# A perceiver layer on one core: transposed router rows kept for the shared network, router logits with 8 moving columns, and an expert product between two shared products

## The chip, the core and the metric

The kernel runs on one core of a Trainium2 chip. Its engines are PE (TensorE: matrix products and transposes, into eight PSUM banks), DVE (VectorE), ACT (ScalarE), POOL (GpSimd) and SP (SyncE, which here issues most DMAs). Each engine works through its own instructions in order and waits for counters (semaphores) that the others raise. The metric is the device time of one execution, in microseconds (us).

## What is computed

The input is x, 32 batches of 64 tokens with 512 features, and a context of 32 x 1601 rows. Three residual blocks follow each other: an attention over the context, a causal self-attention of 16 heads, and a feed-forward block with a router, experts and a shared network. The change touches the third block and its seam with the second:

```python
x = x + xattn(layernorm(x), ctx)
x = x + attn(layernorm(x))
h = layernorm(x)
logits = h @ w_router.T                  # 8 experts
weight, idx = top_k(softmax(logits), 2)  # weights made to sum to 1
moe = sum over the two chosen experts of weight * (square(relu(h @ w1[e].T)) @ w2[e].T)
shared = square(relu(h @ ws1.T)) @ ws2.T # 1024 inner features
out = x + shared + moe
```

## The kernel before

The 2048 tokens are T = 16 tiles of 128. P = 128, D = 512, KD = D / P = 4, KF = 1024 / P = 8, E = 8, TR = 12 and TA = 12. The order of every engine's work is written out by hand; semaphores join them.

Router: for each tile DVE writes the normalised rows to `hs[i]` (line 1027), PE transposes them (`router_T`, line 1912, four transposes recorded at line 1702), ACT copies them from PSUM to `h2Tr[i]`, one of two buffers (`router`, line 833, recorded at line 716), and PE multiplies with the router's weights, stored with 120 columns of zeros (`router`, line 2023, the tile's rows being the stationary operand and 128 columns moving). Tiles TR to T-1 have buffers of their own (`h2T_late`), since the shared network takes them at the very end of the kernel.

Shared network for tiles 0 to 11, in six pairs p: DVE normalises each tile again (`norm_c`), PE transposes it again (`tokens_T_c`), ACT and DVE make high and low parts from PSUM (`h2_high`, `h2_low`). PE computes four groups g of 256 inner features (`shared_first`, 24 records a group) into banks 1 to 4. ACT applies relu (`relu_of`), DVE squares, ACT and DVE split into `shT_p` (`shared_high`, line 921, and `shared_low`, line 1460). PE multiplies with ws2, one tile after the other (`shared_second`, 24 records each), into bank 5 for even tiles and bank 6 for odd ones, and DVE adds the bank to x (`residual_c`, line 1466, counter `x3_ready`). The second half of a pair runs after the first half of the next pair. `shared_second` of a tile waits until `residual_c` of the tile two before has read its bank. ACT's first `shared_high` of pair p waits for `shared_done` >= 2p, since `shT_p` is one buffer.

Between these, DVE computes the routing (lines 1542 to 1604) and the rows are scattered to `moe_in` by POOL (line 697).

Experts: 39 tiles of routed tokens. SP loads a tile's tokens (`load_slots`, line 553, four DMAs), the low parts of w1 and w2 of the tile's expert (`load_low`, line 533; `load_low2`, line 539); the rest of the weights is resident (`load_w1`, `load_w2`) and is loaded while the shared network runs. DVE transposes the tokens (`tokens_T`, line 1529), ACT and DVE split them. On PE `experts(g)` transposes the squared values of tile g-1, makes the first product of tile g (lines 2147 to 2156) and then the second product of tile g-1 (the same lines). On DVE, `tokens_T(g+1)` stands ahead of the square of tile g.

On SP, before: after the last attention product (`out_done`) it loads w1 of experts 2 to 7, then stores h2T of the late tiles, then w1 of expert 1, then x of tiles 0 to 3 and 4 to 7 away (line 519, each followed by weights that take the place), then x of tiles 12 to 15 (line 526); it waits for that store (line 530), loads low parts for tile 0, w1 of expert 0, the tokens of tile 0, six experts' worth of w2 and, once tile 0 is transposed, the tokens of tile 1.

## Time and profile before

| | |
|---|---|
| median of 3 runs | 1371.45 us (1368.12 to 1372.08) |
| profiled execution | 1369.75 us |
| its span, first to last instruction | 1368.0 us |
| PE busy | 1324.4 us, 97% |
| DVE busy | 719.2 us, 53% |
| ACT busy | 341.6 us, 25% |
| granted TensorE clock, mean | 0.995 |
| share of PE in the chain that ended last | 87% |
| share of SP's issue and of DMAs in that chain | 6% and 3% |

All times in the text are microseconds from the start of the span of this profiled execution. PE's busy time is split in products and weight loads (PEld), which overlap. A row of the timeline gives start, duration, engine, line and operation, the operands, the number of instructions merged in it, and in brackets the idle time before it with what ended it. A row of the chain of waits gives start, duration and the work that the end of the span waited for. The granted clock 1.00 is 2.4 GHz and 0.50 is 1.2 GHz.

### The profile page before, as it was taken

The numbers are of one execution on the slowest core, as the hardware profiler recorded it, in microseconds if no ns is written. First come the engines' busy times: TensorE is split into PE (matmuls) and PEld (weight loads), VectorE is DVE, ScalarE is ACT, GpSimd is POOL, SyncE is SP. The second block draws the span as 40 slices with busy tenths as digits, with TensorE's granted clock in tenths as the row PEclk, the third lists the DMA queues.
The fourth block names the chain that finished last, engine by engine and source line by source line (L and its number), as shares of the span: only waits on it lengthen the run. The fifth ranks groups of instructions, "written<-read, shape, count | busy, mean of one in ns | idle before, by whom it ended". The sixth has DMA issues, their size and how long they took to land.

```text
span 1368.0 us, 20895 instructions
## 1 busy us (share of the span) xinstructions
PE 1324.4 (97%) x7251; PEld 818.1 (60%) x7252; DVE 719.2 (53%) x1353; ACT 341.6 (25%) x604; POOL 160.6 (12%) x169
## 2 busy tenths in 40 slices
PE   5889999999999999999999999899998999999999
PEld 2334444444444444357888888799896666666643
DVE  3235444544444444467877786757442444444436
ACT  2101111211111111234444443442121222222210
POOL 0000000000000000003000005502330000000045
PEclk9999999999999999999999999999999999999999
DMA  9999999999999999721466752062549998999887
GB/s 360 392 401 395 396 394 395 395 394 384 383 381 379 379 379 352 297 82 76 157 252 256 271 211 97 35 222 80 192 153 310 295 302 283 298 291 293 273 323 257
DMA packets 122945, 392.18 MB, mean 287 GB/s; under 512 B 12144, under 2 KB 34672, under 8 KB 122768
## 3 DMA queue, kind: packets, MB, share of 16 engines
q1 hardware_dynamic: 117776, 374.79, 75.0%
q0 software_dynamic: 5120, 16.78, 3.4%
q8 instruction: 26, 0.43, 0.1%
q14 instruction: 23, 0.19, 0.0%
HBM read 333.32 MB, written 58.20 MB: 286 GB/s over the span
## 4 chain that ended last, share of the span: by engine, by line
PE 87%; SPq 6%; DMA 3%; DVE 2%; issue 1%; ACT 1%; POOL 0%; DVEq 0%; POOLq 0%; ACTq 0%
PE ps L1801 12%; PE ps L1865 12%; PE ps L1741 10%; PE ps L1855 10%; PE ps L2147 7%; PE ps L1702 4%; PE ps L1762 4%; PE ps L1754 4%; PE ps L1751 4%; PE ps L2153 3%; PE ps L2150 3%; PE ps L2156 3%; PE ps L2222 2%; PE ps L2214 2%; SPq L393 2%; DMA arena<-ctx_t 2%
## 5 line engine op out<-in xcount | busy, mean ns | idle before, releaser
L716 ACT ACTIVATE arena<-ps 128x512 f32<-128x512 f32 (+1 forms) x151 | 79.9, 542 | 602.2 <-PE ps L1702 278.6
L1801 PE MATMUL ps<-arena 128*64 128x512 f32 (+1 forms) x832 | 193.6, 597 | 0.5 <-DMA arena<-ctx_n 0.5
L1741 PE MATMUL ps<-arena 128*64 128x512 f32 (+1 forms) x1024 | 178.9, 503 | 11.9 <-DMA arena<-ctx_t 8.9
L1865 PE MATMUL ps<-split 128*128 128x256 f32 x1344 | 170.1, 285 | 0.1
L1855 PE MATMUL ps<-split 128*128 128x512 f32 x672 | 163.8, 396 | 4.3 <-DVE split L1460 2.3
L1865 PEld LDWEIGHTS ps<-split 128*128 128x128 f32 x1344 | 163.5, 191 | 6.1 <-issue 5.2
L1741 PEld LDWEIGHTS ps<-arena 128*64 128x64 f32 x1024 | 66.3, 137 | 133.1 <-issue 119.9
L1855 PEld LDWEIGHTS ps<-split 128*128 128x128 f32 x672 | 123.1, 188 | 34.4 <-issue 3.1
L1140 DVE SCALAR_TENSOR_TENSOR arena<-arena,hbar 128x512 f32<-128x512 f32 x128 | 90.5, 749 | 94.7 <-PE ps L1762 89.9
L1801 PEld LDWEIGHTS ps<-arena 128*64 128x64 f32 (+1 forms) x832 | 58.4, 138 | 114.4 <-issue 112.2
L1073 DVE TENSOR_REDUCE small<-ps 128x1 f32<-128x1601 f32 x16 | 29.2, 1825 | 141.3 <-PE ps L1741 141.3
L2150 PE MATMUL ps<-split 128*128 x195 | 90.0, 559 | 0.0
L2147 PE MATMUL ps<-arena 128*128 x156 | 73.3, 592 | 0.9 <-ACT split L974 0.9
L1529 DVE STREAM_TRANSPOSE zero<-arena 128x512 uint32<-128x512 uint32 x39 | 27.7, 711 | 81.2 <-PE ps L2156 57.7
L635 POOL COPY arena<-arena 128x512 f32<-128x512 f32 x16 | 9.7, 609 | 495.5 <-PE ps L1723 490.2
L708 POOL DMA_INDIRECT arena<-moe_out,slot_i x32 | 33.2, 1037 | 295.7 <-DMA moe_out<-arena 286.3
L1762 PE MATMUL ps<-arena 128*64 128x512 f32 x256 | 66.0, 594 | 0.0
L1702 PE MATMUL ps<-ident,arena 128*128 128x128 f32 x368 | 54.6, 280 | 10.0 <-DVE arena L1027 9.7
L1751 PE MATMUL ps<-arena 128*128 128x512 f32 x128 | 60.2, 614 | 1.9 <-DMA arena<-w_qv 1.9
L2150 PEld LDWEIGHTS ps<-split 128*128 128x128 f32 x195 | 37.4, 192 | 39.3 <-issue 37.6
L1754 PE MATMUL ps<-arena 128*128 128x512 f32 x128 | 57.6, 593 | 1.9 <-DVE arena L1127 1.9
L2153 PE MATMUL ps<-split 128*128 x195 | 58.3, 397 | 0.0
(180 smaller groups left out, 1681.1 us busy)
## 6 DMA issues: line engine op xcount, KB each, us to landing
arena<-ctx_t SPq DMA_DIRECT2D x128, 800.5 KB, 19.1
arena<-ctx_n SPq DMA_DIRECT2D x128, 768.0 KB, 15.7
split<-parts_low SPq DMA_DIRECT2D x39, 768.0 KB, 7.3
split<-parts_low SPq DMA_DIRECT2D x39, 512.0 KB, 5.2
moe_in<-zero SPq DMA_DIRECT2D x3, 3328.0 KB, 13.5
arena<-moe_in SPq DMA_DIRECT2D x156, 64.0 KB, 3.9
moe_out<-arena SPq DMA_DIRECT2D x39, 256.0 KB, 4.7
stage_raw<-w1t SPq DMA_DIRECT2D x8, 768.0 KB, 5.5
```

The source lines that it names most:

```text
L1140: v.scalar_tensor_tensor(Wc[:, h, :], w_qv_sb[:, 3 * KD + k, :], hbar[:, k, h:h + 1], w_qv_sb[:, k, :], ALU.mult, ALU.add).then_inc(wc_rea ...
L1702: last = nc.tensor.transpose(dst[:, P * k:P * (k + 1)], src[:, P * k:P * (k + 1)], ident[:, :])
L1741: last = mm(bank(n)[S * h:S * (h + 1), 0:w], qT[:, k, S * h:S * (h + 1)], ctxT[h][:, k, at_j:at_j + w], start=(k == 0), stop=(k == KD - 1))
L1751: mm(bank(5), F2[:, k, :], w_qv_sb[:, KD + k, :], start=(k == 0), stop=False)
L1754: mm(bank(5), F3[:, k, :], w_qv_sb[:, 2 * KD + k, :], start=False, stop=False)
L1762: last = mm(bank(5)[r, :], F1[i][:, k, r], Wc[:, h, :], start=False, stop=(k == KD - 1))
L1801: last = mm(bank(7)[S * h:S * (h + 1), :], ET[0:w, c, S * h:S * (h + 1)], ctxN[h][0:w, c, :], start=(c == 0), stop=(c == JC - 1))
L1855: last = mm(dst, lhs[a][:, k, :], rhs[b][:, k, :], start=(k + i == 0), stop=(k == n - 1 and i == 2))
L1865: last = mm(dst[:, 2 * P * m:2 * P * (m + 1)], w[a][:, k, c], tokens[b][:, k, :], start=(k + i == 0), stop=(k == KD - 1 and i == 2))
L2147: mm(dst, raw(k), raw_w(k), start=(k == n), stop=False)
L2150: mm(dst, parts[0][:, k, :], high_w(k), start=False, stop=False)
L2153: mm(dst, parts[1][:, k, :], high_w(k), start=False, stop=False)
```

## The change

What it does, part by part:

- The transposed rows of tiles 0 to 11 are kept: tiles 0 and 1 in `h2T_first`, tiles 2 to 11 in `h2T_rows`, where w1 of experts 2, 3 and half of 4 will lie. `norm_c` and `tokens_T_c` are gone, and `h2_high` and `h2_low` read the kept rows. Pair 1 has buffers of its own for its high and low parts.
- The router's products move 8 columns instead of 128, and the logits of tiles 0 to 11 share bank 3; they are copied out twice instead of four times.
- The router's work for tiles 12 to 15 stands between the groups of the shared network's first pair.
- SP loads w1 of experts 2, 3 and 4 later, one by one: expert 2 after the first store of x, 3 and 4 after the second.
- On PE `experts(0)` comes between the second products of tiles 10 and 11. In tile 11's product (`shared_last`) the passes with the low part of the tokens come first, and then SP may load the next low part of w1 over them. PE waits for all w1 before `experts(0)`.
- On DVE the last pair's squares and subtractions all come ahead of `residual_c` of tile 8; that of tile 9 comes after the transposing of expert tile 0, that of tile 11 after that of expert tile 1.
- On SP the tokens of tile 1 are loaded ahead of the last four w2 instead of behind them, and after the last shared product the tokens of tile 2 are loaded ahead of the low parts of w2.

```diff
+        h2T_first = [within(f"h2T_first{i}", 2 * KD * D + 2 * D + i * D, KD, P) for i in range(2)]
+        h2T_rows = within("h2T_rows", SPLIT, TR - 2, KD, P)
...
-        low_lo = ARENA + TR * D, used[0], used[0] + KA * D
+        low_lo = ARENA + TR * D, 8192 + 9216 - KA * D, used[0]
...
-        def logits(g):
-
-            return bank(3 + 2 * (g % 2))
+        def logits(lo, hi):
+
+            return bank(3 if hi <= TR else 0)[:, E * lo:E * hi]
...
@@ SP
-            load_w1(2, E)
+            load_w1(5, E)
...
                 if i == 0:
+                    sp.wait_ge(h2lo_ready, 6)
+                    load_w1(2, 3)
                     sp.wait_ge(routed, EXPERTS)
                     load_w2(3 * KD * D, 3, 4)
+                else:
+                    sp.wait_ge(h2lo_ready, 10)
+                    load_w1(3, 4)
+                    sp.wait_ge(h2lo_ready, TA)
+                    load_w1(4, 5)
...
             load_slots(0)
             load_w2(0 * KD * D, 0, 2)
+            sp.wait_ge(xgT_ready, 1)
+            load_slots(1)
             load_w2(4 * KD * D, 4, 6)
             load_w2(2 * KD * D, 2, 3)
-            sp.wait_ge(xgT_ready, 1)
-            load_slots(1)
+            e = expert_of(1)
+            sp.wait_ge(shlo_used, 1)
+            load_low(e, 1)
             sp.wait_ge(shared_done, TA)
+            load_slots(2)
             load_low2(0, expert_of(0))
-            load_low(expert_of(1), 1)
-            load_slots(2)
             load_low(expert_of(2), 2)
@@ ACT
             with act.Fori(3, TR // 2 - 1) as n:
                 for i in range(2):
-                    router(2 * n + i, i, False)
+                    router(2 * n + i, i)
+            act.wait_ge(out_done, T)
             for i in range(2):
-                h2_high(0, i, True)
+                h2_high(0, i)
             for i in range(2):
-                router(TR - 2 + i, i, False)
+                router(TR - 2 + i, i)
+            for i in range(2):
+                h2_high(1, i)
             sqrt_of_var(7, TR, T)
             relu_of(0, 0, True)
             relu_of(0, 1, True)
+            for i in range(2):
+                router(TR + i, i, late_bank[i])
             shared_high(0, 0, True)
...
@@ DVE
-            shared(4, norms=False, scatter=6)
-            shared_start(TA // 2 - 1, more=False, norms=False)
+            shared(4, scatter=6)
+            last_pair = TA // 2 - 1
+            square(last_pair, 0)
+            square(last_pair, 1)
+            shared_low(last_pair, 0)
+            square(last_pair, 2)
+            shared_low(last_pair, 1)
+            square(last_pair, 3)
+            shared_low(last_pair, 2)
+            shared_low(last_pair, 3)
+            residual_c(TA - 4, 0)
             dve.wait_ge(slots_zeroed, 48)
-            shared_rest(TA // 2 - 1)
             tokens_T(0)
             tokens_low(0)
-            for i in range(2):
-                residual_c(TA - 2 + i, i)
+            residual_c(TA - 3, 1)
+            residual_c(TA - 2, 0)
...
-            experts(0, True, False, True)
+            experts_square(0)
+            tokens_T(1)
+            tokens_low(1)
+            residual_c(TA - 1, 1)
@@ PE
-            def router(t, i):
+            def router(t):
 
                 pe.wait_ge(r_h2T_ready, t + 1)
-                src = h2T_late[t - TR] if t >= TR else h2Tr[i]
                 for k in range(KD):
-                    last = mm(logits(t // KD)[:, P * (t % KD):P * (t % KD + 1)], src[:, k, :], wr_sb[:, k, :],
+                    last = mm(logits(t, t + 1), h2T_of(t)[:, k, :], wr_sb[:, k, 0:E],
                               start=(k == 0), stop=(k == KD - 1))
                 last.then_inc(lg_done, 1)
...
+            def shared_last(p):
+
+                pe.wait_ge(x3_ready, 2 * p)
+                high, low = (a[:, :, P:2 * P] for a in shT_p)
+                for k in range(KF):
+                    last = mm(bank(6), low[:, k, :], ws2_p[0][:, k, :], start=(k == 0), stop=False)
+                last.then_inc(shlo_used, 1)
...
+            shared_group(0, 0, first=True)
+            shared_group(0, 1, first=True)
+            router_T(TR, 0, False, late_bank[0])
+            router_T(TR + 1, 1, False, late_bank[1])
+            pe.wait_ge(lg_read, 1)
+            shared_group(0, 2, first=True)
+            router(TR)
+            router_T(TR + 2, 0, False, late_bank[0])
+            router(TR + 1)
+            router_T(TR + 3, 1, False, late_bank[1])
+            shared_group(0, 3, first=True)
+            router(TR + 2)
+            router(TR + 3)
+            shared_first(1)
...
-            for i in range(2):
-                shared_second(TA // 2 - 1, i)
-            pe.wait_ge(w1_in, 16 * 6)
+            shared_second(TA // 2 - 1, 0)
+            pe.wait_ge(w1_in, 16 * 12)
             pe.wait_ge(relu_ready, 4 * (TA // 2) - 2)
             experts(0, now=(0, 0))
+            shared_last(TA // 2 - 1)
             experts(1, now=(1, 0), last=0, second=True)
```

## Rows read from the trace of the kernel before

**Rows 1.** The page, busy time, share of span and instructions of each engine.

```profile
PE 1324.4 (97%) x7251; PEld 818.1 (60%) x7252; DVE 719.2 (53%) x1353; ACT 341.6 (25%) x604; POOL 160.6 (12%) x169
```

**Rows 2.** The chain of waits, router stretch: start, duration, what.

```profile
880.57 1.78 PE ps L2023 x16
...
897.08 1.31 PE ps L1702 x12
...
899.28 0.44 PE ps L1702 x4
```

**Rows 3.** The timeline of PE around the first late tile.

```profile
912.91 1.91 PE L1702 MATMUL ps<-ident,arena 128*128 128x128 f32 x16
915.26 1.13 PE L2023 MATMUL ps<-zero,arena 128*128 128x128 f32 x8 [0.45 <-ACT arena L716]
```

**Rows 4.** The chain of waits through the pairs.

```profile
955.26 0.87 PE ps L1702 x8
...
967.03 11.51 PE ps L1865 x96
...
1025.18 10.92 PE ps L1855 x48
```

**Rows 5.** The timeline of weight loads, two windows around the first two of a run.

```profile
871.17 0.30 PEld L2023 LDWEIGHTS ps<-zero,arena 128*128 128x128 f32 x2
...
875.40 0.20 PEld L1702 LDWEIGHTS ps<-ident,arena 128*128 128x128 f32 x2 [1.23 <-DVE arena L1027]
```

**Rows 6.** Stretches: length, busy PE, PEld, DVE, ACT, POOL, clock, DMA share, GB/s.

```profile
873.57:876.98 3.41, 1.57 (x32) 1.19 (x28) 3.38 (x6) 1.65 (x2) 3.33 (x3) 1.00 0.00 0
876.98:880.39 3.41, 3.41 (x16) 3.03 (x16) 3.29 (x5) 1.79 (x3) 3.25 (x4) 0.50 0.00 0
893.10:900.70 7.60, 7.60 (x70) 7.60 (x69) 5.25 (x15) 4.30 (x8) 0.37 (x3) 1.00 0.81 315
1057.88:1061.30 3.42, 3.42 (x8) 2.33 (x7) 0.42 (x1) 0.06 (x1) 0.00 (x0) 0.50 0.72 235
```

**Rows 7.** The timeline of ACT, one copy of transposed rows.

```profile
898.52 0.60 ACT L716 ACTIVATE arena<-ps 128x512 f32<-128x512 f32 x1
```

**Rows 8.** The chain of waits, last shared products and first expert steps.

```profile
1041.67 0.69 DVE split L1460
...
1065.29 0.44 PE ps L1702 x4
...
1071.75 0.44 PE ps L1702 x4
1072.18 0.86 PE ps L2147 x2
...
1075.12 1.72 PE ps L2147 x4
```

**Rows 9.** The timeline of DVE and PE in the same stretch.

```profile
1030.76 0.69 DVE L1466 TENSOR_TENSOR arena<-arena,ps 128x512 f32<-128x512 f32 x1 [8.51 <-PE ps L1855]
...
1037.69 1.62 PE L1855 MATMUL ps<-split 128*128 128x512 f32 x6 [1.60 <-DVE split L1460]
...
1056.59 0.66 PE L1702 MATMUL ps<-ident,row_a 128*128 128x128 f32 x4 [3.55 <-DVE row_a L1640]
```

**Rows 10.** The timeline of SP's queue: issues of token loads.

```profile
1030.31 2.77 SPq L553 DMA_DIRECT2D arena<-moe_in  x4
...
1055.17 1.75 SPq L553 DMA_DIRECT2D arena<-moe_in  x4
```

**Rows 11.** DMAs: low parts of w2 on the page; landing times of line 553.

```profile
split<-parts_low SPq DMA_DIRECT2D x39, 512.0 KB, 5.2
...
DMA to landing us min/median/max: 2.4/5.3/10.5
```

**Rows 12.** SP's waits; last, a stretch with line 1702's busy times, clock, DMA, GB/s.

```profile
SPq L530 <- DMA x_away<-arena: 6.6, 1, 6.6
...
1013.70:1037.00 23.30, 0.00 (x0) 0.00 (x0) 1.00 0.81 277
```

More of the change, by code:

```diff
@@ L219, in perceiver_layer @@
         shT_p = [as_split(carve(KF, 2 * P)) for _ in range(2)]
-        h2T_p = [as_split(carve(KD, 2 * P)) for _ in range(2)]
+        h2T_p = [[as_split(carve(KD, 2 * P)) for _ in range(2)]]
+        h2T_p.append([])
+        for lo in (4 * KD * D, 2 * KD * D + 2 * D):
+            at(lo)
+            h2T_p[1].append(as_split(carve(KD, 2 * P)))
         relu = [row_a[:, :], row_b[:, :]]
@@ L229, in perceiver_layer @@
         hs = [carve(D) for _ in range(2)]
-        h2Tr = [carve(KD, P) for _ in range(2)]
+        carve(2, D)
         assert used[0] == 3 * KD * D, used[0]
@@ L831, in exp_probs, with router @@
                                      ACT.Exp).then_inc(p_ready, 1)
-            def router(t, i, first, source=None):
+            def router(t, i, source=None):
                 act.wait_ge(r_h2T_done, t + 1)
-                if not first:
-                    act.wait_ge(lg_done, t - 1)
-                dst = h2T_late[t - TR] if isinstance(t, int) and t >= TR else h2Tr[i]
-                copy(dst.rearrange("p a b -> p (a b)"), source or bank(1 + i)).then_inc(r_h2T_ready, 1)
+                nc.scalar.activation(h2T_of(t), (source or bank(1 + i)).rearrange("p (k n) -> p k n", n=P), ACT.Copy
+                                     ).then_inc(r_h2T_ready, 1)
             def round_set(n):
@@ L899, in _, with h2_high @@
             for i in range(2):
-                router(4 + i, i, False)
+                router(4 + i, i)
             attn_high(T - 1, 1, False)
-            def h2_high(p, i, first):
-                act.wait_ge(h2T_done, 2 * p + i + 1)
-                if not first:
+            def h2_high(p, i):
+                act.wait_ge(r_h2T_ready, 2 * p + i + 1)
+                if not isinstance(p, int):
                     act.wait_ge(sh_done, 4 * p)
-                nc.scalar.activation(h2T_p[0][:, :, P * i:P * (i + 1)],
-                                     bank(7 * i).rearrange("p (k n) -> p k n", n=P), ACT.Copy).then_inc(h2hi_ready, 1)
+                nc.scalar.activation(h2T_of_pair(p)[0][:, :, P * i:P * (i + 1)], h2T_of(2 * p + i), ACT.Copy
+                                     ).then_inc(h2hi_ready, 1)
             def relu_of(p, g, first=False):
@@ L951, in _ @@
             for i in range(2):
-                h2_high(1, i, False)
-            for t in range(TR, T):
-                router(t, t % 2, False, late_bank[t % 2])
+                router(TR + 2 + i, i, late_bank[i])
             relu_of(0, 3)
@@ L1474, in _ @@
                 router(TR + i, i)
-            copy_logits(2)
             for i in range(2):
-                norm_c(2 + i, i)
+                h2_low(1, i)
             square(0, 0)
             square(0, 1)
+            for i in range(2):
+                router(TR + 2 + i, i)
             shared_low(0, 0)
@@ L1482, in _ @@
             shared_low(0, 1)
-            for i in range(2):
-                h2_low(1, i)
-            for i in range(2):
-                router(TR + 2 + i, i)
             square(0, 3)
@@ L2047, in _ @@
             probs_T(T - 1)
-            router(2, 0)
-            router(3, 1)
+            router(2)
+            router(3)
             attend_b(T - 1, 1)
@@ L2098, in shared_second, with shared @@
                            arrived if i == 0 else None).then_inc(shared_done, 1)
-            def shared(p, second=False, more=True):
+            def shared_last(p):
[4 more added lines that the diff above has]
+                last.then_inc(shlo_used, 1)
+                for k in range(KF):
+                    for part in ws2_p:
+                        last = mm(bank(6), high[:, k, :], part[:, k, :], start=False,
+                                  stop=(k == KF - 1 and part is ws2_p[1]))
+                last.then_inc(shared_done, 1)
+            def shared(p):
                 shared_first(p)
                 for i in range(2):
-                    if more:
-                        tokens_T_c(p + 1, i)
-                for i in range(2):
-                    shared_second(p - 1, i, second)
+                    shared_second(p - 1, i)
             pe.wait_ge(ws1_split, 4 * KD)
-            shared_first(0, first=True)
-            for i in range(2):
-                tokens_T_c(1, i)
-            for t in range(TR, T):
-                if t == TR + 1:
-                    pe.wait_ge(relu_ready, 1)
-                router_T(t, t % 2, False, late_bank[t % 2])
-                if t == TR + 1:
-                    pe.wait_ge(relu_ready, 3)
-                if t > TR:
-                    router(t - 1, 1 - t % 2)
-            router(T - 1, 1)
-            shared_first(1, second=True)
+            shared_group(0, 0, first=True)
[12 more added lines that the diff above has]
+            shared_first(1)
             pe.wait_ge(routed, MASK)
@@ L2136, in _ @@
                 shared(p)
-            shared(TA // 2 - 1, more=False)
+            shared(TA // 2 - 1)
             def expert(g):
```

131 lines of the change are left out of this document (55 added, 76 removed).

## The prediction, made before the changed kernel had run

> **What bounds the kernel now.** I read the page first: PE is busy for 97% of the span [rows 1], so work taken from PE counts wherever no other engine ends the stage. The change touches 870 to 1085 us, so I then read the chain of waits there. To 1036.1 us it is PE nearly without a break: router products and transposes first [rows 2], then per pair of token tiles 96 products of line 1865, 8 transposes and 48 products of line 1855 [rows 4]. A microsecond of PE work removed there comes off the end. From 1036.1 to 1057.4 us the chain leaves PE: first for the split of the last pair's squared values on ACT and DVE, then for a load of expert tokens (line 553). From 1065 us each of the 39 expert tiles takes 6.46 us of PE [rows 8].
>
> **Removed: twelve second transposes.** Every tile of the shared network was normalised and transposed a second time, four transposes in 0.44 us [rows 2]. Two tiles stand in the run of 12 transposes at 897.08, two in the 16 at 912.91, and two, 0.87 us, in each of the next four pairs [rows 2 to 4]. All lie on the chain: 12 x 0.44 = 5.2 us. DVE also loses the second normalisations, off the chain, worth nothing. The rounding copies and subtractions stay, now reading SBUF.
>
> **Reordered: the last four tiles' router work.** It now lies between groups of line 1865. After the 16 transposes at 912.91 PE waited 0.45 us for an ACT copy, and the products that followed took 1.13 us where eight take 0.89 (half of 1.78) [rows 2, 3]: 0.7 us, which 2.88 us of shared products per group (11.51/4 [rows 4]) now cover. So far 5.9 us. Covers: ACT's two rounding copies now stand ahead of its copies of tiles 10 and 11, two more of 0.6 us [rows 7] in a stretch where ACT is busy for 4.3 of 7.6 us [rows 6]; without that cover PE would wait up to 1.2 us. The split of ws1 on POOL ends well before. The routing arithmetic on DVE begins with PE's logits and moves with them, behind 11.5 us of shared products as before.
>
> **Router products with 8 columns instead of 128: nothing.** There are 16 tiles of 8 records, now 0.11 us apart (16 in 1.78 us [rows 2]). Their streaming falls to almost nothing, but each keeps its 128-column weight load. Two such loads at the head of a run took 0.30 us in all and 0.19 each, so the second began 0.11 us after the first, before a product could hold it; two loads for transposes took 0.20 and 0.14, 0.06 apart [rows 5]. A record therefore stays at 0.11 us. Bounds: 0.06 us (the transpose's load) would give 14 x 8 x 0.05 = 5.6 us on the chain (tiles 0 and 1 lie in idle time); the 0.12 us of line 1865 (11.51/96) would cost 1.1. I take nothing: the loads of this very line show the limit.
>
> **TensorE's clock in the router stretch: a loss.** From 893.1 to 900.7 us PE is now busy throughout at the full clock [rows 6]. Afterwards it streams only five tiles' transposes there, 2.2 of 7.6 us, and otherwise loads weights. The clock stood at half, 1.2 GHz, from 877.0 to 880.4 after 3.4 us in which PE was busy for 1.57, and from 1057.9 to 1061.3 after idle time [rows 6, 9]. I expect one fall, with 3.4 us at half rate: 1.7 us lost. Bounds: no fall, or two such stretches (3.4 us lost).
> The Trainium skill ("TensorE: Matmul & The Clock Gate", Part 4) says that transposes do not count as busy for the clock. The trace is against it: from 877.0 to 880.4 PE ran nothing but transposes, and the clock rose at the end of it [rows 6]. By the rule the fall would be sure and hold to the end of the stretch, its second 3.8 us of work taking 7.6, 3.8 us lost; by the row it is only likely.
>
> **The last shared products and the first expert: a loss too.** Before, from 1036.10 to the transposes of the third expert step at 1065.29 is 29.2 us [rows 4, 8]. Afterwards, on the same time axis:
> DVE now runs all squares and subtractions of the last pair ahead of the residual addition of tile 8, which ran at 1030.76, as soon as the bank was full [rows 9]. PE may not write bank 5, tile 10's product, until that addition is done. The chain of squares cannot start sooner than before, since ACT's first copy still waits for both products of pair 4 (1036.1), and DVE's last subtraction ends at 1042.36 [rows 8]. Then 0.69 us of addition: PE starts at 1043.05 instead of 1037.69 [rows 9]. A wait of 6.95 us, with all of PE's later work queued behind it.
> Then: 24 products 5.46 (half of 10.92 [rows 4]); a clock fall, as there was after 3.55 us idle at 1056.59 [rows 6, 9], 1.7; the first expert product 2.94 (1072.18 to 1075.12 [rows 8]), its tokens ready by 1045; tile 11's product 5.46; the second expert step 6.46. Sum 28.97.
> SP then is late. Its token loads for step 3 were issued at 1055.17, before the step that began at 1056.59 [rows 9, 10], and the low parts of the first w2 before them. Now both follow the last shared product, tokens (1.75 us of issue) first, and the low parts, with a register load between, go out about 3 us into the second step. They land 5.2 us after issue [rows 11], at 8.2, where PE wants them at 6.2. Step 3's tokens are delayed alike, and DVE transposes them ahead of the square that PE needs. I take 2.5 us for both (bounds 0.4, if the emptier queues land in 4 us, and 4.5). Result 31.5 against 29.2: 2.3 us lost. The 3.55 us of idle time and 1.9 us of slow clock that expert 0's product now covers are gone; late instead is the bank.
>
> **Weights reloaded later on SP.** The kept rows cover the places of experts 2, 3 and half of 4, so three loads of 1 MB move behind the stores of x. Two are queued ahead of the store whose wait of 6.6 us holds SP [rows 12]. 2 MB at 277 GB/s [rows 12] are 7.2 us, and 1.7 us of issue: the first token loads go from 1030.31 [rows 10] to at most 1039.2 and at the median of 5.3 us [rows 11] land at about 1047, ahead of the first expert product at 1050.2. Hidden, with 1 to 3 us to spare after transpose and split; past that each microsecond costs one.
>
> **Sum.** -5.9 (transposes, waits) + 0 (columns) + 1.7 (clock) + 2.3 (transition) = -1.9 us. Against the profiled 1369.75 that is 1367.9; the median of the runs shown is 1371.45, 1.7 above it, so 1369.5. This kernel's measurement tells 0.3%, 4.1 us, from no change.
>
> **Rivals.**
> A, the clock does not fall in the router stretch. For: the records follow each other as closely as before. -3.6: 1367.8. Chance 0.22; with shorter waits for SP it passes 4.1 in half the cases.
> B, a router record takes 0.06 us. For: two transposes' loads lay so. Against: the two loads of this line did not. -1.9 - 4.8 (of the 5.6, ACT's copies of 0.6 us a tile [rows 7] take some back): 1364.7. Chance 0.10. The same page of the Trainium skill ("Back-to-back issue gap") puts a product of few columns at a floor of 25 ns, by which the gain would be some 9 us, and its section on LDWEIGHTS a 128-column load at 107 ns, by which it is none; the loads above side with the second.
> C, the transition gains: PE does not wait for bank 5, so neither the 2.3 us lost nor the old 5.4 us remain: -9.6, 1361.8. Against: the order of DVE's instructions. Chance 0.08.
> D, the first tokens come late because of the reloaded weights. With the longest landing, 10.5 us [rows 11], they are there at 1052.5, and with transpose and split (1.9) the expert product starts 4.1 us late: +2.2, 1373.7. It decides from a landing at 1048.3 on, is slower than before from 1050.2, and beyond 0.3% from 1054.3. Chance 0.22, half of it beyond.
> The forecast itself has 0.38.
>
> **Numbers.** Faster by over 0.3%: B, C and nearly half of A, 0.28. Slower by over 0.3%: half of D and a little of the forecast with its bounds together, 0.14. Within: 0.58. The range takes in B below and D above: 1364 to 1374.5.
>
> **What would show it.** Pairs from 943 us on take 22.4 us, not 23.3; router records stay 0.11 us apart (B if half); a stretch at 1.2 GHz near 897 to 904 (A if none); PE idle for 7 us before tile 10's product, released by DVE's addition (C if not), a slow stretch behind it; low parts late in the second expert step; the first tokens there before PE asks (D if not). I am wrong altogether if expert steps past the fifth differ from 6.46 us.

## The result, and the profile after

The changed kernel takes 1374.18 us (median of 20 runs, 1368.37 to 1376.14) against 1369.12 for the kernel before (20 runs beside it). The ratio is 1.0032, 95% interval 1.0021 to 1.0043: 4.4 us slower, where 1.9 us faster were forecast. The profiled execution took 1375.11 us, its span is 1373.4 (1368.0 before), its mean granted clock 0.988 (0.995 before). The profiled spans therefore differ by 5.4 us, of which the runs as a whole bear out 4.4.

The page's busy times show nothing of this:

```profile
PE 1324.8 (96%) x7203; PEld 818.7 (60%) x7204; DVE 713.8 (52%) x1339; ACT 342.0 (25%) x604; POOL 160.9 (12%) x169
```

PE is busy for as long as before [rows 1], though it has twelve tiles of transposes less to do. A slow clock stretches what is left, and it counts as busy time. So I went to the chain of waits and to the stretches with their clock. In the changed file the lines have other numbers: the transposes are line 1721 (1702 before), the router's products 2041 (2023), the shared products 1884 and 1874 (1865 and 1855), the residual addition 1483 (1466), the subtraction 1477 (1460), SP's token loads 574 (553), the expert products 2163 to 2172 (2147 to 2156). The changed SP order also has 554 (low part of w1), 560 (low part of w2), 547 (store of x) and 551 (the wait for it).

The chain of waits through the router stretch, to be read beside [rows 2, 3]:

```profile
876.90 2.09 PE ps L1721 x8
...
880.70 3.21 PE ps L2041 x16
...
885.87 2.75 PE ps L1721 x12
888.63 2.77 PE ps L1874 x12
...
896.78 0.79 PE ps L2041 x8
897.57 0.49 PE ps L1721 x4
...
903.65 5.85 PE ps L1884 x48
```

From 890 us on a tile of 8 router records takes 0.79 us and the four transposes behind it 0.49, together 1.28; before they took 0.89 and 0.44. But the first 16 records took 3.21 us and 12 transposes 2.75, twice their time at full clock. The stretches around them show it (length; busy time and instructions of PE, PEld, DVE, ACT, POOL; granted clock; DMA share, GB/s):

```profile
871.44:874.85 3.41, 2.87 (x49) 2.70 (x48) 3.34 (x4) 0.91 (x3) 3.33 (x4) 1.00 0.02 5
874.85:878.26 3.41, 2.47 (x10) 1.81 (x11) 3.38 (x7) 1.73 (x3) 3.25 (x4) 0.50 0.00 0
878.26:881.68 3.42, 3.42 (x19) 3.42 (x17) 2.09 (x3) 2.19 (x4) 3.26 (x5) 0.50 0.00 0
881.68:885.09 3.41, 3.41 (x33) 3.38 (x35) 0.00 (x0) 0.00 (x0) 1.04 (x1) 0.50 0.00 0
885.09:888.50 3.41, 3.41 (x29) 3.29 (x26) 1.04 (x4) 1.19 (x2) 0.00 (x0) 0.50 0.00 0
888.50:891.92 3.42, 3.42 (x20) 2.90 (x20) 2.09 (x4) 0.60 (x1) 0.00 (x0) 1.00 0.02 5
...
898.74:902.16 3.42, 3.42 (x35) 3.42 (x34) 1.84 (x3) 2.39 (x6) 0.00 (x0) 1.00 1.02 422
...
1035.28:1045.52 10.24, 5.57 (x13) 4.41 (x14) 5.67 (x9) 2.68 (x5) 0.00 (x0) 0.50 1.03 375
1045.52:1048.93 3.41, 3.41 (x15) 2.49 (x14) 0.60 (x1) 0.00 (x0) 0.00 (x0) 1.00 1.11 323
...
1076.23:1079.65 3.42, 3.42 (x7) 1.99 (x7) 0.42 (x1) 0.20 (x1) 0.00 (x0) 0.50 0.83 254
```

The clock stands at half for 13.65 us from 874.85 on, where it stood there for 3.4 before [rows 6], and for 10.24 us from 1035.28. The chain through the last pairs and the first expert steps, to be read beside [rows 4, 8]:

```profile
943.35 11.51 PE ps L1884 x96
954.86 10.91 PE ps L1874 x48
965.77 11.51 PE ps L1884 x96
...
1022.12 10.92 PE ps L1874 x48
...
1039.30 0.61 DVE arena L1483
1039.95 8.34 PE ps L1874 x24
...
1053.08 3.64 PE ps L2118 x16
1056.74 0.33 SPq L574
...
1059.26 4.32 DMA split<-parts_low
...
1066.65 6.99 DMA arena<-moe_in
1073.73 0.71 DVE zero L1534
...
1075.08 0.66 PE ps L1721 x4
...
1083.97 0.44 PE ps L1721 x4
1090.47 0.44 PE ps L1721 x4
```

and PE's timeline there, with the idle time and its releaser in brackets:

```profile
1039.95 8.34 PE L1874 MATMUL ps<-split 128*128 128x512 f32 x24 [6.92 <-DVE arena L1483]
...
1063.62 0.73 PE L2172 MATMUL ps<-split 128*128 128x512 f32 x2 [0.91 <-DMA split<-parts_low]
...
1075.08 0.66 PE L1721 MATMUL ps<-ident,row_a 128*128 128x128 f32 x4 [3.85 <-DVE row_a L1645]
```

The balance of the two profiles has three stations:

| | before | after | difference |
|---|---|---|---|
| first shared group (line 1865 / 1884) begins | 901.56 | 903.65 | +2.1 |
| pair 4's products end | 1036.10 | 1033.04 | -3.1 |
| from there to the transposes of expert tile 5 | 48.6 | 57.4 | +8.9 |

The difference at the second station holds that of the first, so the saved transposes brought 5.2 us between the two. The 8.9 us can be cut once more, at the transposes of tile 2, the prediction's third step. Where PE does not wait in front of them, PE's timeline has the start of transposes 0.16 us ahead of the chain's (before: 1065.13 and 1065.29), so both kernels are taken from the timeline here: up to tile 2 (1064.19, before 1065.13) it is 31.15 us against 29.03, +2.1, and from there to tile 5 (1090.31, before 1084.51) it is 26.1 against 19.4, +6.7. Behind tile 5 both kernels go on at 6.5 us a tile. In what follows "the seam" is the third line of the table, a length of one profile from the end of pair 4's products to the transposes of expert tile 5, with the tiles counted from 0 (tile 0's product lies at 1048.29, the transposes of tiles 1 to 5 at 1056.55, 1064.19, 1075.08, 1083.97 and 1090.47). The seams given below for the experiments are all read from PE's timeline; there the changed kernel has 57.3 us and the kernel before 48.4.

SP's timeline and its waits show what SP did meanwhile:

```profile
1018.53 0.43 SPq L547 DMA_DIRECT2D x_away<-arena  x1
1033.34 0.35 SPq L554 DMA_DIRECT2D split<-parts_low  x1
...
1056.74 1.76 SPq L574 DMA_DIRECT2D arena<-moe_in  x4
1059.26 0.37 SPq L560 DMA_DIRECT2D split<-parts_low  x1
...
1065.28 1.79 SPq L574 DMA_DIRECT2D arena<-moe_in  x4
```
```profile
SPq L551 <- DMA x_away<-arena: 13.4, 1, 13.4
```

SP now waits 13.4 us for the store of x behind 2 MB of w1, against 6.6 [rows 12].

### The profile page after: what moved, and what is told of

Same layout as the page of the kernel before. It is cut to its first block, busy times and chain, and to the rows that moved or that the text cites. A ratio compares the mean times of both kernels' runs of the same rounds, so it can differ in the third digit from the quotient of the medians.

```text
span 1373.4 us, 20759 instructions
## 1 busy us (share of the span) xinstructions
PE 1324.8 (96%) x7203; PEld 818.7 (60%) x7204; DVE 713.8 (52%) x1339; ACT 342.0 (25%) x604; POOL 160.9 (12%) x169
## 4 chain that ended last, share of the span: by engine, by line
PE 87%; SPq 6%; DMA 3%; DVE 2%; issue 1%; ACT 1%; POOL 0%; DVEq 0%; POOLq 0%; ACTq 0%
PE ps L1884 12%; PE ps L1820 12%; PE ps L1760 10%; PE ps L1874 10%; PE ps L2163 7%; PE ps L1721 4%; PE ps L1781 4%; PE ps L1773 4%; PE ps L1770 4%; PE ps L2166 3%; PE ps L2169 3%; PE ps L2172 3%; PE ps L2238 2%; PE ps L2230 2%; SPq L407 2%; DMA arena<-ctx_t 2%
## 5 line engine op out<-in xcount | busy, mean ns | idle before, releaser
L739 ACT ACTIVATE arena<-ps 128x512 f32<-128x512 f32 (+1 forms) x135 | 70.6, 535 | 586.5 <-PE ps L1721 262.3
L1874 PE MATMUL ps<-split 128*128 128x512 f32 x648 | 160.3, 401 | 8.9 <-DVE arena L1483 6.9
L2166 PE MATMUL ps<-split 128*128 x195 | 90.0, 559 | 0.0
L1721 PE MATMUL ps<-ident,arena 128*128 128x128 f32 x320 | 50.5, 290 | 9.5 <-DVE arena L1051 9.5
L2172 PE MATMUL ps<-split 128*128 128x512 f32 x195 | 57.6, 392 | 0.9 <-DMA split<-parts_low 0.9
```

Source lines behind the costliest of these rows:

```text
L1721: last = nc.tensor.transpose(dst[:, P * k:P * (k + 1)], src[:, P * k:P * (k + 1)], ident[:, :])
L1874: last = mm(dst, lhs[a][:, k, :], rhs[b][:, k, :], start=(k + i == 0), stop=(k == n - 1 and i == 2))
L2166: mm(dst, parts[0][:, k, :], high_w(k), start=False, stop=False)
L2172: last = mm(dst, parts[0][:, k, :], low_w_of[:, k, :], start=False, stop=(k == n - 1))
```

## Theories and experiments

Two things had to be told apart. First, whether the 8-column router products are what lets the clock fall for 13.7 us. Second, what lengthened the seam by 8.9 us: PE's wait for the bank at 1033 (my prediction's step), or SP, which is held by the moved loads of w1 and by its new order. Every ratio below is against the kernel before, run beside the experiment in five rounds (5 to 12 runs of each experiment), with its 95% interval.

**The clock.** The changed kernel with 128 columns again, all else kept:

```diff
-                    last = mm(logits(t, t + 1), h2T_of(t)[:, k, :], wr_sb[:, k, 0:E],
+                    last = mm(bank(3 if t < TR else 0)[:, E * t:E * t + P], h2T_of(t)[:, k, :], wr_sb[:, k, 0:P],
```

> The changed kernel with the router's products moving 128 columns again (neighbouring tiles' zero columns overlap in the bank, each tile's own eight are written last). Theory, the narrow products let TensorE's clock fall: the stretch at 1.2 GHz from 874.9 to 888.5 us shrinks to about the 3.4 us of the kernel before, the first shared group starts some 2 to 3 us earlier than at 903.65, router records go from 0.099 back to 0.111 us apart (14 x 8 x 0.012 = 1.3 us lost), and the time falls by 1.5 to 2.5 us. Rival, the clock fell because of where its looks happened to lie and the narrow products have no part in it: the slow stretch stays in the profile or comes and goes, and the time rises by 1.3 us.

1369.2 us, ratio 1.0006 (0.9996 to 1.0015): 3.6 us less than the changed kernel by the ratios, and by the two intervals roughly 1.6 to 5.5. The two profiles differ by more, 7.4 us of span: 3.5 up to the first shared group (900.17 instead of 903.65) and 3.9 in the seam (53.4 us instead of 57.3), though nothing in the seam was edited. So a seam differs by some 4 us from profile to profile, and only the runs say what a change is worth. The other way round, the kernel before with 8 columns and nothing else changed:

```diff
-                    last = mm(logits(t // KD)[:, P * (t % KD):P * (t % KD + 1)], src[:, k, :], wr_sb[:, k, :],
+                    last = mm(logits(t // KD)[:, P * (t % KD):P * (t % KD) + E], src[:, k, :], wr_sb[:, k, 0:E],
```

> The kernel before with the router's products moving 8 columns and nothing else. Theory, clock: a slow stretch of 10 to 14 us from about 875 us instead of 3.4 us, router records 0.099 us apart, the first shared group 1 to 2.5 us later than at 901.56, and the time 1 to 2.5 us longer. Rival, narrow products are harmless: the time 1.3 us shorter by the closer records.

1371.39 us, ratio 1.0018 (1.0008 to 1.0028): 2.5 us more. The same stretch of the four kernels, before, changed, before with 8 columns, changed with 128 columns:

```profile
876.00:890.00 14.00, 13.01 (x108) 11.67 (x108) 9.24 (x20) 5.14 (x9) 6.41 (x7) 0.88 0.01 1
```
```profile
876.00:890.00 14.00, 13.70 (x86) 12.63 (x85) 6.07 (x14) 4.78 (x8) 6.48 (x7) 0.55 0.00 1
```
```profile
876.00:890.00 14.00, 13.70 (x86) 12.71 (x85) 6.07 (x14) 4.79 (x8) 6.18 (x7) 0.56 0.01 1
```
```profile
876.00:890.00 14.00, 13.44 (x110) 12.25 (x111) 7.73 (x16) 4.67 (x8) 5.46 (x6) 0.88 0.00 1
```

In these four the clock goes with the number of columns: 0.55 and 0.56 with 8, 0.88 and 0.88 with 128. PE is "busy" for 13.7 us in the slow ones and gets through 86 records instead of 108 or 110. The profiles of all kernels of this case, those of the experiments below among them, say the same of the whole router stretch, 870 to 910 us:

| columns moved | profiles | time at 1.2 GHz |
|---|---|---|
| 8 | 6 | 13.65 us in four, 10.24 in two |
| 64 | 1 | 3.41 us |
| 128 | 7 | 3.41 us in six, none in one |

With 8 columns the slow time lies in one piece (from 874.85 in the changed kernel, from 874.68 in the kernel before with 8 columns) or in two, a short one before 882 and another from 896 to 902 on. The piece of the kernel with the early addition (described below) starts where the prediction looked for it:

```profile
897.50:907.74 10.24, 10.24 (x50) 10.24 (x50) 4.58 (x16) 3.96 (x7) 0.00 (x0) 0.50 0.47 188
```

Both directions agree, so this cause is shown; the two pairs put it at 2.5 us (1.1 to 3.8) and 3.6 us.

A third width, 64 columns (`0:64` in the same line of the changed kernel):

> The changed kernel with 64 moving columns in the router's products. Theory, what holds the clock is how much PE streams, and 64 columns keep half of it: the slow stretch between 875 and 904 us is mostly the 3.4 us of the kernel before, as with 128 columns, while the records are 0.10 us apart as with 8: 3 to 5 us under the changed kernel. Rival, only the full 128 columns keep the clock: within 1.5 us of the changed kernel.

1370.14 us, ratio 1.0003 (0.9982 to 1.0025), 4.0 us under the changed kernel by the ratios, though the two intervals just overlap. The clock fell for 3.4 us, from 879.7, as with 128. (The profiled execution was the slowest of the twelve, 1375.13 us; its router stretch lies some 3 us later than in the changed kernel's profile, a delay that is there before the first router record.) On the chain a tile's eight records took

```profile
890.78 0.84 PE ps L2041 x8
```

So in the one profile 64 columns keep the clock like 128, and they stand between 0.79 us with 8 columns and 0.89 with 128 for the tile. That the time is better than with 128 columns can't be told: the one interval lies within the other.

**The bank.** The residual addition of tile 8 moved ahead, so that DVE frees the bank before it works off the last pair:

```diff
             square(last_pair, 1)
+            residual_c(TA - 4, 0)
             shared_low(last_pair, 0)
...
             shared_low(last_pair, 3)
-            residual_c(TA - 4, 0)
```

> The changed kernel with DVE's residual addition of tile 8 before the last pair's subtractions instead of behind them. Theory, PE waits for the bank: its wait of 6.92 us ahead of tile 10's product shrinks to the 2.3 us of the kernel before, the slow stretch from 1035.3 to 1045.5 us mostly goes (2.9 us lost in it), and the time falls by 4.5 to 7.5 us. Rival, the expert loads of SP set the seam: PE reaches the third expert step sooner but waits there for tokens by as much more, and the time falls by less than 2 us.

1373.08 us, ratio 1.0032 (1.0021 to 1.0044): as slow as the changed kernel. The wait of 6.92 us was gone, yet PE's timeline shows another in its place, and the chain what released it:

```profile
1061.44 1.65 PE L2172 MATMUL ps<-split 128*128 128x512 f32 x3 [6.09 <-DMA split<-parts_low]
```
```profile
1055.23 8.90 DMA split<-parts_low
```

Before tile 0 PE also waited 1.51 us for the first tokens. In tile 1 it asked for expert weights' low parts, which SP had issued late and which took 8.9 us to land behind other loads. The seam was 54.4 us, 2.9 shorter than in the changed kernel's profile, which is within what seams differ by and which the runs as a whole don't show.

**The whole old seam.** The changed kernel with the old order of PE, DVE and SP from the last pair on, but with the w1 loads where the change puts them (PE's part is shown; DVE's and SP's lines go back in the same way):

```diff
-            shared_second(TA // 2 - 1, 0)
+            for i in range(2):
+                shared_second(TA // 2 - 1, i)
...
-            shared_last(TA // 2 - 1)
             experts(1, now=(1, 0), last=0, second=True)
```

> The changed kernel with the seam of the kernel before: both last shared products ahead of the first expert product, DVE's and SP's order there as before; kept rows, narrow router products and the later w1 loads stay. Theory, the seam lost 8.9 us of what the removed transposes gave: from the end of pair 4 to the fifth expert step 48.6 to 50 us instead of 57.4, and the time falls by 7 to 9 us against the changed kernel, to 3 to 4 us under the kernel before. Rival, the w1 loads that moved behind the stores of x are what makes the tokens late: the seam stays over 53 us and the time falls by less than 4 us.

1371.03 us, ratio 1.0031 (1.0019 to 1.0043). (The ratio takes in all runs; seven of the eleven lie near 1371 us and four near 1375, so by the median alone it would be 1.0020, and a gain of some 2 us over the changed kernel isn't ruled out.) PE no longer waited for the bank, but before expert tile 1, for tokens (the seam was 54.6 us):

```profile
1060.63 1.12 PE L1713 MATMUL ps<-ident,row_a 128*128 128x128 f32 x4 [9.58 <-DVE row_a L1637]
```

The chain has their transfer, behind the last issue, here and in the kernel before:

```profile
1049.42 9.78 DMA arena<-moe_in
```
```profile
1044.67 10.48 DMA arena<-moe_in
```

They did not travel longer than before. They left later: 15.3 us after the end of pair 4's products (1034.10 here), where it was 8.6 before. That is 6.7 us more, and SP's wait for the store had grown by 7.0 (13.6 us, before 6.6).

Neither the bank nor the new order is thus the one cause. What these two runs share with the changed kernel is the place of the w1 loads.

**Late w1 loads alone**: in the kernel before, w1 of experts 3 and 4 goes behind the second store and its w2, as the change has it (PE's wait for w1 is raised to match):

```diff
-            load_w1(2, E)
+            load_w1(2, 3)
+            load_w1(5, E)
...
+                else:
+                    load_w1(3, 4)
+                    load_w1(4, 5)
```

> The kernel before with the w1 loads of experts 3 and 4 moved from after the attention to behind the second store of x and its w2, ahead of the third store, and nothing else. Theory, they delay the whole seam: SP's wait for the third store doubles to about 13 us, the tokens of tile 1 come 7 us later, PE waits 9 to 10 us instead of 3.55 ahead of the second expert step, and the time rises by 5 to 9 us. Rival, the loads are hidden: the time stays within 1.5 us.

1375.14 us, ratio 1.0049 (1.0036 to 1.0061): 6.8 us slower for two loads of 1 MB each, without any other part of the change (seam 54.0 us). SP's wait and PE's:

```profile
SPq L534 <- DMA x_away<-arena: 12.6, 1, 12.6
```
```profile
1062.60 1.11 PE L1706 MATMUL ps<-ident,row_a 128*128 128x128 f32 x4 [9.63 <-DVE row_a L1644]
```

**The same two loads taken back, in the changed kernel**: w1 of experts 3 and 4 is loaded behind the first store of x, not the second, under the same waits for the rows that lie there:

```diff
                     load_w2(3 * KD * D, 3, 4)
-                else:
                     sp.wait_ge(h2lo_ready, 10)
                     load_w1(3, 4)
```

> The changed kernel with the w1 loads of experts 3 and 4 issued as soon as their places are free, between the two stores of x, instead of behind the second store and ahead of the third. Theory, these 2 MB hold the third store and with it all of SP's seam: SP's wait for that store falls from 13.4 to about 6.6 us, the first low part goes out some 7 us before the end of pair 4's products instead of with it, PE's wait of 3.85 us ahead of the third expert step and the slow stretch behind it go, and the time falls by 2 to 5 us; the 6.9 us wait for the bank stays, so it does not fall by more. Rival, the order of the loads behind the last shared product makes SP late: the time falls by less than 1 us.

1373.21 us, ratio 1.0040 (1.0027 to 1.0052): no gain. SP was in time again: it waited 6.4 us for the store, and the first low part went out at

```profile
1024.36 0.35 SPq L553 DMA_DIRECT2D split<-parts_low  x1
```

where it was 1033.34 in the changed kernel. But PE's wait for the bank stayed at 6.93 us, and a wait of 3.56 before tile 3 with it: on SP the tokens of tiles 2 and 3 are loaded only once the last shared product has ended, and this product stands behind the bank on PE. The seam was 57.2 us. So each delay hides the other's removal. The test is to take both away.

**Both at once**, the early loads and the early addition, 8 columns and the new order kept:

```diff
                     load_w2(3 * KD * D, 3, 4)
-                else:
...
             square(last_pair, 1)
+            residual_c(TA - 4, 0)
...
             shared_low(last_pair, 3)
-            residual_c(TA - 4, 0)
```

> The changed kernel with both edits that did nothing alone: early w1 loads and the residual addition of tile 8 ahead of the subtractions. Theory, the wait for the bank and the late loads overlap, each of them enough to hold the seam, so that only taking both away pays: from the end of pair 4 to the fifth expert step 49 to 51 us instead of 57.4 and a time 6 to 8 us under the changed kernel, 1.5 to 3 us under the kernel before. Rival, a third wait stands behind the two: less than 3 us under the changed kernel.

1367.73 us, ratio 0.9986 (0.9962 to 1.0011), some 6 us below the changed kernel. Its waits in the seam:

```profile
1036.11 3.02 PE L1873 MATMUL ps<-split 128*128 128x512 f32 x12 [0.36 <-DVE split L1476]
...
1051.74 0.96 PE L2171 MATMUL ps<-split 128*128 128x512 f32 x3 [1.52 <-DMA split<-parts_low]
...
1065.38 0.66 PE L1720 MATMUL ps<-ident,row_a 128*128 128x128 f32 x4 [0.86 <-DVE row_a L1644]
```

The four corners, with 8 columns throughout:

| | addition late (as changed) | addition early |
|---|---|---|
| w1 late (as changed) | 1.0032, seam 57.3 | 1.0032, seam 54.4 |
| w1 early | 1.0040, seam 57.2 | 0.9986, seam 48.4 |

The seam of the last cell is 5.0 us shorter than the shortest of three profiles in which nothing of the changed seam was touched (57.3, and 53.4 and 55.4 with 128 and 64 columns); the other three cells can't be told apart by their seams.

**Is the new order worth anything, once the rest is mended?** Early loads and 128 columns, with the old order of the seam, and with the new one (addition early, low parts of w2 ahead of the tokens of tile 2 on SP). Beside the edits shown above, the second has on SP

```diff
             sp.wait_ge(shared_done, TA)
-            load_slots(2)
             load_low2(0, expert_of(0))
+            load_slots(2)
```

> The changed kernel with early w1 loads, the seam of the kernel before and 128 moving columns: of the change only the kept rows and the reordered router work are left. Theory: 5.2 us of transposes and 0.7 us of waiting are saved and nothing is given back, 5 to 6.5 us under the kernel before (ratio about 0.996); from the end of pair 4 to the fifth expert step 48.6 us. Rival, something else in the kept rows or the moved loads costs: less than 3 us under it.

> The changed kernel with early w1 loads, the residual addition of tile 8 ahead of the subtractions, the low parts of the first w2 ahead of the tokens of tile 2, and 128 moving columns; the expert product stays between the two shared products. Theory: with all three costs removed the placement gives what it was for, PE loses only the 2.3 us ahead of tile 10 and up to 2 us of late low parts, 44 to 46.5 us from the end of pair 4 to the fifth expert step, and 7 to 10 us under the kernel before (ratio 0.993 to 0.995). Rival, SP's chain of one low part waiting for the one before still comes late behind the last shared product: no better than the seam of the kernel before, 5 to 6 us under.

Old order: 1363.29 us, ratio 0.9960 (0.9947 to 0.9974), seam 47.3 us. New order: 1363.92 us, ratio 0.9963 (0.9949 to 0.9977), seam 47.0. The expert product between the last two shared products is worth nothing that can be measured, while the kept rows and the reordered router work are worth 5.5 us. With the old order PE's wait before tile 1 is 1.86 us (3.55 before, [rows 9]):

```profile
1047.76 0.66 PE L1712 MATMUL ps<-ident,row_a 128*128 128x128 f32 x4 [1.86 <-DVE row_a L1636]
```

**Two smaller questions.** The kernel of the four corners' last cell with 128 columns, SP's order as in the change:

```diff
-                    last = mm(logits(t, t + 1), h2T_of(t)[:, k, :], wr_sb[:, k, 0:E],
+                    last = mm(bank(3 if t < TR else 0)[:, E * t:E * t + P], h2T_of(t)[:, k, :], wr_sb[:, k, 0:P],
```

> The same with 128 moving columns, that is, the kernel with early w1 loads, early residual addition and 128 columns but SP's order behind the last shared product as changed (tokens of tile 2 ahead of the low parts of the first w2). Theory, that order costs what the low parts are late, 0.5 to 2 us of PE wait in the second and third expert step: ratio 0.997 to 0.998 where the run with the other order had 0.9963. Rival, the order is indifferent: the same ratio as there within 0.0005.

1365.92 us, ratio 0.9973 (0.9946 to 1.0001), waits of 1.65 and 2.22 us, seam 49.4. The interval overlaps both that with 8 columns and that with the other SP order, so what SP's order costs is not told apart here. Last, the old order with the tokens of tile 1 loaded ahead of w2 of experts 4 and 5:

```diff
+            load_w2(2 * KD * D, 2, 3)
             sp.wait_ge(xgT_ready, 1)
             load_slots(1)
             load_w2(4 * KD * D, 4, 6)
-            load_w2(2 * KD * D, 2, 3)
```

> Kept rows, reordered router work, 128 columns, early w1 loads and the seam of the kernel before, with one step of the change's SP order: the tokens of expert tile 1 loaded ahead of w2 of experts 4 and 5. Theory, PE's wait of 1.86 us ahead of the second expert step goes, since those tokens no longer stand behind 2 MB: 0 to 2 us under the same kernel without this step (ratio 0.9945 to 0.996). Rival, the low parts of w1 for tile 1, which waited for the last shared product, are late instead and nothing is won.

1364.26 us, ratio 0.9954 (0.9932 to 0.9977). The wait for tokens fell from 1.86 to 1.41 us, and one for low parts grew from 0.39 to 1.64:

```profile
1053.79 0.98 PE L2163 MATMUL ps<-split 128*128 128x512 f32 x3 [1.64 <-DMA split<-parts_low]
```

Not distinguishable from the order without it. Three kernels with early loads and 128 columns, at 0.9960, 0.9963 and 0.9954, are thus faster than both kernels of this case.

## Why the prediction was wrong

**Twelve transposes less, -5.2, and 0.7 of waits: right.** The pairs take 22.4 us (943.35 to 965.77 on the chain), and the first two stations hold -6.3 us beside the 3.2 of slow clock, where -5.9 and some 0.7 from the records (next point) were there to be had. At the end of the kernel it shows as 5.5 us where nothing eats it (ratio 0.9960).

**8 columns change nothing in a record: nearly right.** The time of a run of records is set by its weight loads, which stay 0.11 us apart, and rival B falls. What there is to gain is 0.05 us per tile and its transposes (1.28 against 1.33), about 0.7 us over 14 tiles, and a little less, since two tiles in a row gain it only once (1.69 us for 16 records instead of 1.79). The Trainium skill ("TensorE: Matmul & The Clock Gate", "Back-to-back issue gap") would have given some 9 us, an estimate by its floor for few columns, which the section states for a product by itself, with no weight load counted; this case's trace doesn't bear that out for products that each load 128 columns of weights.

**The clock in the router stretch, 1.7: right in kind, mis-sized.** It cost 2.5 us (8 columns alone) to 3.6 (by the changed kernel with 128 columns), in the profile 3.2: from 876.90 to the products at 888.63 are 11.7 us, where before were 8.5. I had looked for it near 897 to 904, where the records run in a row with transposes. In the changed kernel's profile it fell at 874.85, in the first tiles; a fall near 897 stood in four of the six profiles with 8 columns (10.2 us from 897.5 with the early addition, 10.2 from 897.8 with the old seam, 6.8 from 896.1 with both mended, 3.4 from 901.4 with the early loads), beside one in the first tiles. My bound of two stretches, 3.4 us lost, was about what it costs. The step that failed is taking one fall of 3.4 us from [rows 6] as the size: that fall had been measured with 128-column products on either side of it, and no row had 8-column products while the clock stood at half. They lengthened it to four times that. That the clock rose at 888.50 behind a stretch with 2.63 us of transposes in 3.41 (from 885.87 on) is a second case, if a weaker one than that of [rows 6], against the Trainium skill's rule (same page, Part 4) that transposes don't count for the clock in the same way.

**The wait for bank 5, 6.95: right** (6.92), and so is its place, its releaser and the slow clock behind it. That slow clock was taken at 1.7 and cost 2.9: 24 products in 8.34 us instead of 5.46. It stayed at half for 10.24 us, over the idle time and on until 1045.52, not for one stretch of 3.4. In the profiles with 128 and 64 columns it was 6.83 us behind the same wait.

**SP late, 2.5 (bounds 0.4 to 4.5): the term that was mis-sized most, and by its place.** The sum was made up to the third step, tile 2, and up to there it was nearly met: 31.3 us as the chain counts, where 31.5 were forecast, with 1.2 us for SP in tile 1 (7.6 us instead of 6.5, 0.91 of it waiting for low parts) and the 1.2 us more of slow clock. But I let the sum end there and took it that from then on every step has its 6.46 us. It has not: from the transposes of tile 2 to those of tile 3 are 10.9 us, 4.4 too many, 3.85 of them the wait for tile 3's tokens, and from there to tile 4's are 8.7, 2.3 too many, since the clock fell once more behind that wait (the stretch at 1076.23). These two are the +6.7. The queue shows why: before, the tokens of tile 3 were issued 24.3 us after the end of pair 4's products (1060.36 on SP's timeline); now 32.2 (1065.28), since all of tokens, low parts of w2 and of w1 first follow the last shared product one by one. They landed 8.4 us after the first of the four issues, 7.0 after the last (median of one issue before 5.3, [rows 11]). Against 2.5, SP's lateness with the clock behind it thus cost 1.2 + 6.7 = 7.9 us, beyond my upper bound. The same count (tiles 1 to 4, less three times 6.46) gives 4.3 to 9.9 us in the eight profiles with the new order of the seam, and 4.5 in that of the changed kernel with 128 columns. The term was close to my upper bound or beyond it everywhere, and a single profile doesn't give it closer than that.

**The reloaded w1 is hidden: wrong, though rival D did not come true as described.** The first tokens were transposed from 1041.80 on and PE asked for them at 1048.29, as predicted. But they were in time only because PE stood at the bank: with the wait taken away (early addition) PE stood 1.51 us for the first tokens and 6.09 us for SP's low parts. I priced the moved loads by their first victim, the first tokens, and not by everything else that SP issues behind the store's completion. In the kernel before they cost 6.8 us all by themselves. Rival D had the right culprit and the wrong place and price. Its chances did not fit its own figures either: its longest landing gives +2.2 us, yet half of its 0.22 was put beyond 4.1. And the sum of the seam has the first tokens "ready by 1045", where the paragraph on the weights has them land at about 1047.

**The sum.** The forecast was -5.9 + 1.7 + 2.3. That 1374.18 us still lies within my 1364 to 1374.5 is luck: the range was drawn for other cases, and the transition cost +8.9 in the profile instead of +2.3. The profile has +2.1 up to the first shared group (3.2 of clock less 1.1 of transposes and records there), -5.2 from there to the end of pair 4, and +8.9 in the seam: +5.8 by these stations, 5.4 by the spans; the seam's part is that of one profile. No rival had the case that came: two waits in parallel, bank and SP, each long enough to hide the other. That is why three experiments that take out one of them (1.0032, 1.0031, 1.0040) show no gain, and the one that takes out both shows 6 us.

**What stays open.** Why the slow clock lies in one piece from 874.85 in one profile, and in two, the second near 897, in another of the same code up to there, was not settled; nor why seams with the same code differ by 4 us. Nor was what SP's order of tokens and low parts is worth. Each seam rests on a single profile.

## What to carry to other kernels

When a store's completion is waited for on a queue, price every load moved ahead of it by all that the queue issues behind the wait, not by the first transfer that follows. When a stage is lengthened, list all waits that end near one another before undoing one: with two in parallel, each single repair measures as zero, and only the pair of them shows its worth. Shortening the moving operand of a product whose weight load sets the pace gains little and can cost the clock; in the one profile taken, 64 columns kept the clock that 8 lost. And before a length of one profile is called an effect, compare it in profiles that don't differ there: here the same seam came out at 53.4 to 57.3 us.

## What the runs showed of the hardware

- **Columns and the clock.** With 8-column router products, each with a 128-column weight load, TensorE stood at 1.2 GHz for 13.65 us (four profiles) or 10.24 us (two) of the router stretch, though PE was busy throughout by its records in most of it (3.41 of 3.41 us from 881.68, 10.24 of 10.24 from 897.50); with 128 columns for 3.41 us in six profiles and not at all in one, with 64 for 3.41 in one.
- **Overlap at the ends of a run.** A tile of 8 router records took 0.79, 0.84 and 0.89 us with 8, 64 and 128 columns, though loads within it stay 0.11 us apart; the four transposes behind took 0.49 instead of 0.44 with 8 columns. Two tiles in a row, 16 records, took 1.69 us with 8 columns and 1.79 with 128, so the columns show once per run of records, not per record.
- **Scatter goes with the clock, loosely.** Of the changed kernel's 20 runs those at 1368.37, 1369.88 and 1371.08 us had a mean clock of 0.994, 0.993 and 0.994, and those at 1375 and above 0.987 to 0.989; between them lie 1370.31 at 0.990 and 1372.98 at 0.987.
- **Loads ahead of a store that is waited for.** Two loads of 1 MB ahead of the store of x lengthened SP's wait for it from 6.6 us to 12.6 to 13.7 (six profiles). The tokens of tile 1 then left later but landed no more slowly: 9.8 us behind the last issue (old seam), 10.5 in the kernel before.
- **Landing behind other loads.** 512 KB of low parts issued 7.6 us behind the last w2 load took 8.9 us to land (early addition); the same load 12.9 us behind it took 4.3 (changed kernel).
